# Embedding tiles transposed in five blocks and stored by field and dimension

## What is computed

```python
B, M, D = 1024, 39, 16            # batch, fields, dimension; S1 = S2 = 128
e = jnp.stack([tbl_f[ids[:, f]] for f in range(39)], axis=1)      # (B, M, D)
x1 = relu(einsum('bhd,bmd,shm->bsd', e,  e, W1) + b1)             # (B, 128, D)
x2 = relu(einsum('bhd,bmd,shm->bsd', x1, e, W2) + b2)             # (B, 128, D)
z  = concatenate([x1.sum(-1), x2.sum(-1), dense_ctx], 1)
y  = relu(relu(z @ W_top1 + b_top1) @ W_top2 + b_top2) @ W_top3   # (B, 1)
```

## Time and profile before

| | us |
|---|---|
| median of 3 runs | 1255.2 |
| lowest and highest | 1251.39 and 1255.94 |
| the profiled execution, its own time | 1253.83 |
| its span, first to last instruction | 1252.0 |
| TensorE busy | 1155.7 (92%) |
| VectorE busy | 928.8 (74%) |
| ScalarE busy | 796.9 (64%) |
| GpSimd busy | 848.6 (68%) |

### The profile page before, as it was taken

The page is one execution under the profiler, slowest core; times in us unless marked ns, Lnnn a source line. Parts: engine busy times, 40 slices in busy tenths (PEclk is TensorE's granted clock), DMA queues, the critical chain, the costliest instruction groups (busy, mean ns, idle before and its releaser), DMA issues.

```text
span 1252.0 us, 17389 instructions
## 1 busy us (share of the span) xinstructions
PE 1155.7 (92%) x4556; PEld 849.7 (68%) x4556; DVE 928.8 (74%) x2846; ACT 796.9 (64%) x2702; POOL 848.6 (68%) x956
## 2 busy tenths in 40 slices
PE   0069999999999999999999999999999999999996
PEld 0037777777777777777776567777777776776775
DVE  2028878887878878788887468888887888774786
ACT  3026766667667766667666466777666666664683
POOL 7725777877787777787786467777777773442455
PEclk9989999999999999999999999999999999999997
DMA  5145666666765666677666267666665676642541
GB/s 163 41 103 106 125 148 130 142 129 134 172 123 119 123 151 125 128 142 151 145 140 121 44 138 156 136 119 124 144 125 124 137 158 133 139 100 62 119 92 35
DMA packets 66346, 154.85 MB, mean 124 GB/s; under 512 B 13219, under 2 KB 18981, under 8 KB 66246
## 3 DMA queue, kind: packets, MB, share of 16 engines
q0 software_dynamic: 28272, 85.81, 36.9%
q1 hardware_dynamic: 37974, 67.92, 22.0%
HBM read 58.59 MB, written 4.20 MB: 50 GB/s over the span
## 4 chain that ended last, share of the span: by engine, by line
POOL 43%; DMA 23%; issue 20%; PE 10%; another core or an unknown queue 2%; ACT 1%; SPq 1%; DVE 0%; POOLq 0%; ACTq 0%; DVEq 0%
DMA prod<-prod 19%; POOL emb L255 15%; POOL tree L284 11%; PE bank L564 7%; POOL tree L291 5%; POOL prod L266 5%; POOL tree L296 3%; POOL a_sum L305 3%; PE l_acc L548 2%; DMA z<-e_shifted 2%; DMA emb_rep<-emb 1%; DMA e_shifted<-e_t 1%; SPq L224 1%; ACT prod L363 0%
## 5 line engine op out<-in xcount | busy, mean ns | idle before, releaser
L363 ACT ACTIVATE prod<-bank,emb 128x128 f32<-128x128 f32 x2560 | 728.6, 372 | 368.8 <-PE bank L564 346.8
L470 DVE SCALAR_TENSOR_TENSOR acc<-bank,emb,acc 128x128 f32<-128x128 f32 x2176 | 613.3, 345 | 138.8 <-PE bank L564 118.4
L564 PE MATMUL bank<-w2h,x1h 128*128 128x512 f32 (+1 forms) x1280 | 537.0, 420 | 5.7 <-DVE x1l L436 4.5
L564 PE MATMUL bank<-w2l,x1h 128*128 128x512 f32 (+1 forms) x1280 | 499.7, 390 | 0.0
L564 PE MATMUL bank<-w2h,x1l 128*128 128x512 f32 (+1 forms) x1280 | 473.6, 433 | 0.0
L255 POOL DMA_INDIRECT emb<-tbl,idx x312 | 309.0, 990 | 82.0 <-issue 77.8
L564 PEld LDWEIGHTS bank<-w2h,x1h 128*128 128x128 f32 x1280 | 242.3, 189 | 119.2 <-issue 54.0
L564 PEld LDWEIGHTS bank<-w2h,x1l 128*128 128x128 f32 x1280 | 241.1, 188 | 87.5 <-issue 35.1
L266 POOL DMA_DIRECT2D prod<-prod x127 | 123.9, 975 | 243.7 <-ACT prod L363 239.7
L284 POOL TENSOR_TENSOR tree<-prod 128x640 f32<-128x640 f32 x128 | 239.3, 1870 | 66.5 <-DMA prod<-prod 66.4
L564 PEld LDWEIGHTS bank<-w2l,x1h 128*128 128x128 f32 x1280 | 241.8, 189 | 60.1 <-issue 17.5
(11 more groups left out here) (75 smaller groups left out, 299.7 us busy)
## 6 DMA issues: line engine op xcount, KB each, us to landing
prod<-prod POOLq DMA_DIRECT2D x127, 640.0 KB
z<-e_shifted SPq DMA_DIRECT2D x160, 234.0 KB
emb_rep<-emb SPq DMA_DIRECT2D x8, 936.0 KB
z<-e_shifted SPq DMA_DIRECT2D x96, 78.0 KB
emb<-tbl,idx POOLq DMA_INDIRECT x312
z<-e_shifted SPq DMA_DIRECT2D x32, 156.0 KB
e_shifted<-e_t SPq DMA_DIRECT2D x32, 128.0 KB, 2.8
prod<-w_by_h SPq DMA_DIRECT2D x3, 832.0 KB
```

Of the source, the lines that this page charges most:

```text
L363: last = nc.scalar.activation(prod[:, ct % P_RING, i, n * S:(n + 1) * S], bank[:, (ct * NB + k) % RING, n * S:(n + 1) * S], ACT.Copy, scal ...
L470: nc.vector.scalar_tensor_tensor(dst, src, scale, dst if step else b2_row[:, :], ALU.mult, ALU.add).then_inc(v_step, 1)
L564: last = nc.tensor.matmul(out_bank[:, 0:b - a], x, w[:, a:b], start=(n == 0), stop=(n == 2))
```

## The change

- The 39 x 16 = 624 columns of a tile of `emb` are transposed once per tile, in blocks of 128 columns = 8 fields x 16 dimensions. `lift(tile, half)`: half 0 is four blocks (fields 0 to 31) into `misc`, half 1 is the last block (112 columns, fields 32 to 38). `emb_rep` is gone.
- ScalarE copies both halves to `e_t` (`copy_lifted(tile, half)`). SP stores them to a DRAM tensor `e_rows`, laid out as (field, dimension, batch), with fields 0 to 18 written twice so that shifted rows can be read past field 38: four transfers per tile (`store_rows`). A field's row is 8 KB (`ROW`), a chunk's part of it 2 KB.
- Both factors are now loaded from there. `load_shifted` has three more transfers per chunk, of 39 x 512 each, that fill a slot `NF` of `z` with the unshifted factor; ScalarE copies that slot to the PSUM tile `e_rep` (`copy_rep(f)`, 117 x 512).
- The halves stand at g = 10 and 15 (copies at 12 and 17) of the third chunk of the tile before; `copy_rep(f + 1)` stands at g = 26, where the lift's copy stood at 30. The loads of chunk f no longer wait for anything of chunk f itself unless it begins a tile: they wait for the contraction of chunk f - 2.
- The gathers get two semaphores per slot, for fields 0 to 31 and 32 to 38, and stand two `ct` earlier.

```diff
+EARLY = 32
+ROW = D * P
-LIFT_AT = 28
-LIFT_COPY_AT = 30
+LIFT_AT = (10, 15)
+LIFT_COPY_AT = (12, 17)
+REP_AT = 26
...
-            return min((TILES - 1) * M, -(-M * (ct + 7) // 16))
+            return min((TILES - 1) * M, -(-M * (ct + 9) // 16))
...
-            def replicate(tile):
...
+            def store_rows(tile):
+                r = tile % 2
...
+                sp.wait_ge(et_ready, 2 * tile + 1)
+                sp.dma_start(rows_at(tile, 0, [[P, P], [8 * ROW, 4], [1, P]]), e_t[:, 0:4, :]).then_inc(et_stored[r], 16)
+                sp.dma_start(rows_at(tile, M, [[P, P], [8 * ROW, 2], [1, P]]), e_t[:, 0:2, :]).then_inc(et_stored[r], 16)
+                sp.dma_start(rows_at(tile, M + 16, [[P, 48], [1, P]]), e_t[0:48, 2, :]).then_inc(et_stored[r], 16)
+                sp.wait_ge(et_ready, 2 * tile + 2)
+                sp.dma_start(rows_at(tile, 32, [[P, 112], [1, P]]), e_t[0:112, 4, :]).then_inc(et_stored[r], 16)
...
             def load_shifted(f):
+                tile, q = divmod(f, CPT)
                 r = f % 2
-                sp.wait_ge(et_ready, f + 1)
...
-                sp.dma_start(shifted[r].ap(), e_t[0:64, r, :]).then_inc(et_stored[r], 16)
-                sp.wait_ge(et_stored[r], 16 * (f // 2 + 1))
+                sp.wait_ge(et_stored[tile % 2], 64 * (tile // 2 + 1))
                 wait(sp, f_used, NF * (f - 1))
+                wait(sp, rep_ready, f - 1)
...
+                for h in range(KP):
+                    first = bass.AP(tensor=e_rows[tile % 2], offset=q * CH, ap=[[ROW, M], [1, CH]])
+                    sp.dma_start(z[h * M:(h + 1) * M, r, NF, :], first).then_inc(in_rep[r], 16)
...
+            def copy_rep(f):
+                act.wait_ge(in_rep[f % 2], 48 * (f // 2 + 1))
+                wait(act, f_made, NF * f)
+                nc.scalar.copy(e_rep[0:KP * M, :], z[0:KP * M, f % 2, NF, :]).then_inc(rep_ready, 1)
...
             def make_f(f, t):
                 rows = F_ROWS[t]
-                dve.wait_ge(lifted, f + 1)
+                dve.wait_ge(rep_ready, f + 1)
...
+            def lift(tile, half):
+                slot = tile % E_SLOTS
+                if half:
+                    wait_late(pe, tile)
+                    pe.wait_ge(et_ready, 2 * tile + 1)
+                    nc.tensor.transpose(misc[0:112, 0:P], emb[:, slot, 4 * P:], ident_f[:, :]).then_inc(lifted, 1)
+                    return
+                wait_early(pe, tile)
...
+                for k in range(4):
+                    last = nc.tensor.transpose(misc[:, k * P:(k + 1) * P], emb[:, slot, k * P:(k + 1) * P],
                                                ident_f[:, :])
                 last.then_inc(lifted, 1)
```

More of the change, by code:

```diff
@@ L131, in build @@
         back_stage = bank[:, 3:5, :].rearrange("p r n -> p (r n)")[:, 0:NF * S]
-        shifted = [nc.dram_tensor(f"e_shifted{r}", (64, CH), F32) for r in range(2)]
+        e_rows = [nc.dram_tensor(f"e_rows{r}", ((M + NK - 1) * ROW,), F32) for r in range(2)]
         in_idx0, in_idx, in_ident = sem("in_idx0"), sem("in_idx"), sem("in_ident")
@@ L138, in build @@
         out_done = sem("out_done")
-        in_rep = sem("in_rep")
+        in_late = [sem(f"in_late{s}") for s in range(E_SLOTS)]
+        in_rep = [sem(f"in_rep{r}") for r in range(2)]
         et_stored = [sem(f"et_stored{r}") for r in range(2)]
@@ new lines, in store_rows @@
+            def store_rows(tile):
+                r = tile % 2
+                if tile >= 2:
+                    for k in range(len(Z_GROUPS)):
+                        sp.wait_ge(in_z[1][k], 48 * 2 * (tile - 1))
+                    sp.wait_ge(in_rep[1], 48 * 2 * (tile - 1))
+                sp.wait_ge(et_ready, 2 * tile + 1)
[4 more added lines that the diff above has]
+                sp.dma_start(rows_at(tile, 32, [[P, 112], [1, P]]), e_t[0:112, 4, :]).then_inc(et_stored[r], 16)
@@ L341, in _, with copy_lifted @@
             act.wait_ge(in_small, 16 * 9)
-            def copy_lifted(f):
-                act.wait_ge(lifted, f + 1)
-                if f >= 2:
-                    act.wait_ge(et_stored[f % 2], 16 * (f // 2))
-                nc.scalar.copy(e_t[0:KP * M, f % 2, :], e_rep[0:KP * M, :]).then_inc(et_ready, 1)
+            def copy_lifted(tile, half):
+                act.wait_ge(lifted, 2 * tile + half + 1)
+                if tile and not half:
+                    act.wait_ge(et_stored[(tile - 1) % 2], 64 * ((tile - 1) // 2 + 1))
+                if half:
+                    nc.scalar.copy(e_t[0:112, 4, :], misc[0:112, 0:P]).then_inc(et_ready, 1)
+                else:
+                    nc.scalar.copy(e_t[:, 0:4, :], misc[:, :].rearrange("p (k n) -> p k n", k=4)).then_inc(et_ready, 1)
+            def copy_rep(f):
+                act.wait_ge(in_rep[f % 2], 48 * (f // 2 + 1))
+                wait(act, f_made, NF * f)
+                nc.scalar.copy(e_rep[0:KP * M, :], z[0:KP * M, f % 2, NF, :]).then_inc(rep_ready, 1)
             def end_layer1(f):
@@ L396, in mlp_tail @@
                 nc.scalar.copy(y[0:1, B - P:], tail3[0:1, :]).then_inc(tail_act, 1)
-            copy_lifted(0)
+            copy_lifted(0, 0)
+            copy_lifted(0, 1)
+            copy_rep(0)
             for c in range(-1, CHUNKS):
@@ L403, in _ @@
                         end_layer1(f)
-                    if f + 1 < CHUNKS and g == LIFT_COPY_AT:
-                        copy_lifted(f + 1)
+                    if c >= 0 and c % CPT == 2 and c // CPT + 1 < TILES and g in LIFT_COPY_AT:
+                        copy_lifted(c // CPT + 1, LIFT_COPY_AT.index(g))
+                    if f + 1 < CHUNKS and g == REP_AT:
+                        copy_rep(f + 1)
                     if c in BATCH_IN:
@@ L528, in _ @@
             pe.wait_ge(in_ident, 16)
-            def lift(f):
-                tile, q = divmod(f, CPT)
-                pe.wait_ge(in_rep, 16 * (tile + 1))
-                wait(pe, f_made, NF * f)
-                wait(pe, et_ready, f)
-                by_d = emb_rep[:, :, :].rearrange("p r (f d) -> p d (r f)", d=D)
-                for d in range(DC):
-                    last = nc.tensor.transpose(e_rep[0:KP * M, d * P:(d + 1) * P], by_d[:, q * DC + d, :],
+            def lift(tile, half):
+                slot = tile % E_SLOTS
+                if half:
+                    wait_late(pe, tile)
[3 more added lines that the diff above has]
+                wait_early(pe, tile)
+                wait(pe, et_ready, 2 * tile)
+                wait(pe, mlp_act, MLP_STEPS * sum(c < CPT * tile - 2 for c in BATCH_IN))
+                for k in range(4):
+                    last = nc.tensor.transpose(misc[:, k * P:(k + 1) * P], emb[:, slot, k * P:(k + 1) * P],
                                                ident_f[:, :])
@@ L621, in mlp_tail @@
                 last.then_inc(tail_mm, 1)
-            lift(0)
+            lift(0, 0)
+            lift(0, 1)
             for c in range(-1, CHUNKS):
```

46 lines of the change are left out of this document (24 added, 22 removed).

## The result

The changed kernel takes 1221.97 us (median of 4 runs, 1218.08 to 1223.72) beside 1253.97 us for the kernel before (4 runs, 1251.39 to 1255.94). The ratio is 0.975, 95% interval 0.9724 to 0.9775: faster by 2.2 to 2.8%. The profiled run took 1218.08 us, 1216.3 of it span, where before had 1253.83 and 1252.0. So the profile explains 35.7 us, 5.4 less than the 41.1 of the forecast's sum. By the medians the gain is 32.0 us: the profiled run is the fastest of the four.

What follows compares the result with a forecast made beforehand. TensorE's stream was taken as the bound from about 83 us on. The terms -21.6 + 7.0 - 25 + 0 + 2 - 3.5 = -41.1 took the span from 1252.0 to 1210.9, own time 1212.7, predicted 1213 us; range 1203 to 1232.

Steps and rivals of the forecast that it cites:

- Step 1: Thirty per-chunk transpose groups (lifts) leave TensorE between the first and last chunk marks, 0.72 us each: -21.6 us.
- Step 2: Block transposes added on TensorE for seven tiles, four at 0.72 us and a single one at 0.28: +7.0 us.
- Step 3: Stalls from VectorE's late shifted rows and the wait for `emb_rep` in the loop mostly vanish: -25 us, bounds -12 and -30.9.
- 4, copy to PSUM: `copy_rep` on ScalarE is as long as the old copy and fits where ScalarE idles: 0 us.
- Step 5: At a tile's first chunk ScalarE may wait for unshifted rows; the ring of banks may cover it: +2 us, bounds 0 to +26.
- Step 6: At the start, first load 5.5 us earlier, 2.0 us more of unshifted loads ahead: -3.5 us, bounds -5.5 and +2.
- Step 7: Transfers and gathers: bytes about equal, the same 312 gathers two `ct` earlier: 0 us.
- The 30.9 us: Stalls forecast between first and last chunk marks: 1117.5 us less 1052.5 stall-free and 34.1 for the MLP batches.
- Rival B: ScalarE's `copy_rep` comes 3.7 us late at each tile's first chunk and the ring gives nothing: 1237 us; chance 0.06.
- rival C: Loads of rows 8 KB apart take twice as long, late at start and tiles' first chunks: 1244 us; with like mishaps 0.04.
- A: VectorE takes over the stalls, over half of step 3 (15 us) comes back: 1228 us, 1221 to 1236; chance 0.14.
- D: SP, running in order, still holds back a chunk's loads in `store_rows`; only steps 1 and 2 count: 1239 us; chance 0.02.

## Why the prediction came out as it did

The time was in the range and 9 us over the 1213 forecast; against the profiled run's 1218.08 it is 5.4 over 1212.7. The other 3.9 are the distance from the profiled run to the median; the forecast named 1.4 us for that and didn't add them. Term by term, from the marks:

| step | forecast | measured |
|---|---|---|
| 1, lifts removed | -21.6 | 30 x (33.24 - 33.95) = -21.3 |
| 2, block transposes | +7.0 | +3.9 |
| 3, stalls (what remains of the 30 chunks) | -25 | -17.2 |
| 4, copy to PSUM | 0 | 0, no wait of TensorE behind it |
| 5, a tile's first chunk | +2 | 0 |
| 6, start to the first mark | -3.5 | -5.3 |
| 7, gathers two steps earlier | 0 | +4.7 in the first chunk |
| behind the last mark | 0 | -0.5 |
| sum | -41.1 | -35.7 |

**Step 1 was right**: 0.71 us between the shortest ordinary chunks, 0.72 forecast (most chunks of the changed kernel take 33.3 to 33.6 us; what that adds is in step 3). The runs with spare transposes show its mechanism from the other side, less sharply: a group added to TensorE's stream lengthened the chunks by 0.3 to 0.4 us, most of its 0.44.

**Step 2 was priced by the wrong row.** The forecast took the block transposes for "the same kind" as the lift. They read adjacent columns, and their weights load in 140 ns (128 columns) and 131 (112), not 287. The changed kernel, third chunk of the first tile:

```profile
161.09 0.60 PE L577 MATMUL misc<-ident_f,emb 128*128 128x128 f32 x4
161.53 1.02 PE L588 MATMUL l_acc<-z,w 117*128 117x512 f32 x2
...
166.74 0.27 PE L571 MATMUL misc<-ident_f,emb 128*112 128x128 f32 x1
...
167.09 0.40 PE L604 MATMUL bank<-w2h,x1h 128*128 128x512 f32 x1
```

The four cost 161.53 - 161.09 = 0.44 us, the single one 167.09 - 166.74 - 0.23 = 0.12 (0.28 forecast), and 7 x 0.56 = 3.9. The third chunks of a tile take 33.9 to 34.1 us, 0.6 over the median of the others.

**Step 3 is the term that failed.** Its mechanism stands: the waits for `z` are gone, and late loads bring them back. Its size fell short, 17.2 for 25, because of what was called a stall. The 30.9 us were what remained when 34.1 us had been put down to the MLP batches by a price per matmul. But the four chunks that hold the batches take 761.57 - 670.94 = 90.6 and 1199.82 - 1114.44 = 85.4 us before and 743.84 - 653.46 = 90.4 and 1164.58 - 1079.52 = 85.1 after. Before, that is 40.2 us over four stall-free chunks, not 34.1; after, it is 42.5 over four of the shorter ones, 0.56 of it one tile's block transposes. So 6.1 us of the 30.9 weren't there to be gained (VectorE did wait for `z` in these chunks before, 0.95, 2.75 and 2.29 us, and with the waits gone they are as long), and of the lifts taken out of them 1.7 us came back. The 90.4 and 85.1 stand within 0.1 us in all three profiles of the changed kernel. How much of it is work and how much the waits between the MLP's own layers wasn't tried. In the 26 other chunks the stalls were 24.6 us and are 5.6 now, a gain of 19.0, inside the bounds. No multiplication waits for loads in the 5.6; most of it is that a usual chunk takes 33.4 us and not 33.24, for which no run has the reason. Two chunks of the kernel before, of 39.8 and 37.7 us, hold 9.7 of the 24.6: in each a stall was followed by a fall of the clock. Of the first of them, 1037 to 1041 us; the granted clock is the third number from the end:

```profile
1037.00:1041.00 4.00, 4.00 (x13) 3.34 (x12) 2.18 (x4) 2.52 (x9) 1.70 (x2) 0.57 0.10 20
```

TensorE had stood still for 2.3 us for `emb_rep` just ahead of it. A clock of 0.57 means the lower of its two levels, 1.2 GHz in place of 2.4, for most of this window. In the second, TensorE had waited 1.8 us for a multiplication that itself waited 4.5 us for `z`. The changed kernel has no slice under 0.9 but the last.

**Step 5 was right in its lean to the cover.** ScalarE's copy waits up to 1.53 us for the unshifted rows, TensorE not at all. Rival B, and the price of rival C, are out.

**Step 6 came out by the forecast's mechanism and something it didn't see.** The first unshifted load was issued at 55.73 (56.3 forecast), and the first mark came 5.3 us earlier where 3.5 were taken. The last six contractions, before and after:

```profile
70.19 7.75 PE L548 MATMUL l_acc<-z,w 117*128 117x512 f32 x12 [2.50 <-issue]
```

```profile
65.92 8.43 PE L588 MATMUL l_acc<-z,w 117*128 117x512 f32 x12 [2.68 <-DVE z L466]
```

They end at 77.94 and 74.35, 3.6 us earlier, as forecast. The other 1.7 are luck: the relu ran 3.06 us behind that end before and 1.36 after. On the second chip, without the delay, it ran at 73.98, 0.03 behind it. The forecast had read the whole 11.5 us up to the relu as twelve passes at a low clock; 3.06 of them were late news, the same delay that then made step 7 wrong.

**Step 7 had the one surprise.** The forecast said "The gathers are the same 312, two `ct` earlier: 0", and looked at their number only. Two `ct` earlier is four gathers more ahead of the first product transfer, and in the start nothing is hidden. Shown by runs: four fewer bring the first bank 5.7 and 5.6 us earlier on two chips; issuing the loads of chunk 1 later doesn't change it; on a third chip the changed kernel has no such delay in its profile and takes 1209.8 us. Only argued is the way it works: that completions of TensorE's matmuls stand behind the gathers' traffic. SP's issuing, half as fast in the same stretch, belongs to what an explanation has to cover.

**The rivals.** A fell: the chunks differ by under 1 us, and TensorE's wait for VectorE's banks went down from 21.7 to 11.9 us, 4.4 of them in the start. C: in the loop VectorE finds every shifted row in place, at rows 8 KB apart, and in the start ScalarE copies the unshifted rows 3.4 us after the first of their loads was issued (55.73 to 59.10), not 18.6. The Trainium skill ("DMA: Bandwidth & Descriptors", section "Latency and other measured facts") tells of a loss only at far larger row distances, 2 MiB and more, and has no figure for 8 KB. The trace agrees as far as it goes: no wait shows a loss. D fell with the same row of waits: the loads run ahead.

The best version found is the changed kernel with 18 opening gathers: 1214.24 and 1214.28 us on two chips, ratios 0.9663 (0.9627 to 0.97) and 0.9695 (0.9653 to 0.9737), 6.7 us under the changed kernel where both ran on one chip. On the chip without the delay it wasn't run; there the changed kernel as it is takes 1209.79 us, ratio 0.9687.

## What to carry to other kernels

Before a remainder is called stalls, take the special chunks out and measure them by their own marks; a price per instruction multiplied up was 6 us short here, and the gain was promised on the remainder. Where a row says that an engine began late, see when the work it waited for had ended before the whole is put down to a slow clock. Price a transpose by one that reads the same pattern, since the step and the width of the source are in it. And when the opening takes on a few more queued operations, count them on the path, though in the steady part they are hidden: here four gathers were worth 6.7 us on one chip, and on another there was no delay to win back.

## What the runs showed of the hardware that was not expected

- Weight loads for fp32 transposes took 140 ns for 128 adjacent columns, 131 for 112, 180 for 117, 206 for 128 elements 28 bytes apart, and 287 for 117 elements 64 bytes apart. A group of four of them cost 0.44, 0.45, 0.48 and 0.72 us of TensorE's stream at 140, 180, 206 and 287 ns.
- On two chips, and in the first profile of the changed kernel, the results of TensorE reached VectorE late (8.4 us behind the end of the bank there) while a train of 61 gathers at 1.25 us each was in its last part: until 88.3 to 88.8 us with the last gather issued at 78.1, and until 83.0 with four fewer. SP took 11.1 to 11.8 us to issue nine loads while the gathers ran. On another chip with the same program SP took 5.2, there was no delay in any of three profiles, and the time was 1209.8 in place of 1221 us.
